# A two-layer pixel-scatter layer on one core: the index stage's lists searched in half rows, its passes fused, some moved to ScalarE

## The chip, the cores and the metric

One Trainium2 chip, one core. The time is the device time of one execution in microseconds, the median of the runs named. Lower is better.

## The reference

Input x is (4, 64, 400, 400), float32. Two layers of the same form follow one another, with their own 1x1 weights. Of one layer:

```python
center = einsum('nchw,oc->nohw', feature, w_center)          # 2 maps
step = relu(einsum('nchw,oc->nohw', feature, w_step))        # 2 maps
prob = sigmoid(einsum('nchw,oc->nohw', feature, w_prob))     # 1 map
offset = transpose(center * step, (0, 2, 3, 1))
th = minimum(round(gh[None] + offset[..., 0]), h - 1)
tw = minimum(round(gw[None] + offset[..., 1]), w - 1)
tgt = mod((th * w + tw).reshape(n, h * w).astype(int32), h * w)
sample = vmap(lambda idx: grid_flat.at[idx].set(grid_flat))(tgt)
sampled = grid_sample_bilinear(feature, scaled(sample))
proped = sampled * prob + feature * (1 - prob)
out = feature * prob + proped * (1 - prob)
```

Each pixel names a target; a target keeps the last pixel that names it, a pixel that nobody names keeps itself. A pixel whose kept source is not itself is called moved. The output is feature + z (sampled - feature) with z = prob (1 - prob).

## The kernel before, in words

The images go in pairs, two images of 64 channels on 128 partitions. A pair of one layer is numbered u = 0 to 3. For each u three things are done. *Tabling* turns the pixels into rows of channels in a table in HBM (TensorE transposes at L1333, ScalarE copies them out at L1397), blends the grid lines that rounding moves (columns on VectorE or GpSimd at L1049 to L1062, rows on VectorE at L1121 to L1139), and computes the five 1x1 maps (L1319). *Indexing*, `indices(u, cuts)`, turns the maps into sources. *Mixing* loads the sampled pixels, transposes them back (L1293), subtracts the feature (L1283) and has VectorE multiply by z and add (L1103, L1105), one image row at a time. Six sweeps run one after another:

| stage | mixes | tables | indexes | from us | to us |
|---|---|---|---|---|---|
| 0 | - | 0 | - | 0 | 545 |
| 1 | - | 1 | 0 | 545 | 1500 |
| 2 | 0 | 2 | 1 | 1500 | 2960 |
| 3 | 1 | 3 | 2 | 2960 | 4640 |
| 4 | 2 | - | 3 | 4640 | 6380 |
| 5 | 3 | - | - | 6380 | 7465 |

A sweep goes over 50 tiles of 8 image rows. The index work of an engine is a Python generator: after each image row of the sweep the engine's program takes `pace` steps of it (0.5, 1, 1.15, 1.15 in stages 1 to 4), so the order on each queue is fixed when the program is built, and work that takes fewer steps ends at an earlier image row. `piece` is one instruction and a step; `pieces(op)` is `cuts` instructions with a step after each (one over 3200 elements in stage 1, two over 1600 in stages 2 to 4); `blanks(n)` is n empty steps; `step` is an instruction without a step of the generator. Every such instruction raises s_v, and the next waits for it.

The index work of one u on VectorE, in order:

- the gate, L483 to L490: z from the last map (Sigmoid and Square on ScalarE, L787 and L790), split into three bfloat16 parts that ScalarE then stores;
- the targets, L493 to L526: maps to target rows and columns, number of the target, distance from the pixel; `code` for targets within R rows and columns (R is 1 in layer 0 and 5 in layer 1), s1m for those further off;
- the near search, L541 and L548, with TensorE, and the far search, a loop on the chip of as many rounds as the fullest partition needs (L578, L579, L622 and others);
- the join, L657 to L676: one source for each pixel. In layer 0 (`sparse`) all moved pixels go to the rounds below;
- in layer 1 the *selection*, L690 to L703: the moved pixels of each image row are picked into 128 slots, eight by eight, the ones that themselves moved away first, by MAX and MATCH_REPLACE. ScalarE and TensorE make row lists and masks of them;
- what is left goes to `keys(1)` and a loop of rounds (L745 on), at the end of which stands the mark "moved"; behind it GpSimd gathers the moved pixels (L916), stores them, and puts them at their places in the table (L940).

If a pixel that itself moved away is left over, a flag makes GpSimd copy the whole table. Behind "moved" VectorE takes over the column blends from GpSimd for a time (`owned`). SyncE issues the first loads of the next stage once `s_path` says that GpSimd is done (L1205 on). In stages 4 and 5 GpSimd also fetches the listed pixels of each image row (L1249), VectorE masks them (L1083), and ScalarE makes one-hot rows (L1431, L1436) beside the gate copy (L1422).

## Time and profile before

| what | value |
|---|---|
| median of 3 runs | 7504.88 us (7486.66 to 7507.91) |
| profiled execution, its own time | 7467.07 us |
| its span | 7465.5 us |
| busy: TensorE, VectorE, ScalarE, GpSimd | 68%, 71%, 41%, 55% |
| TensorE's mean granted clock | 0.834 |

Engines are named PE (TensorE), PEld (its weight loads), DVE (VectorE), ACT (ScalarE), POOL (GpSimd), SP (SyncE). L12 is line 12 of the kernel before. A busy time is the time in which an engine had an instruction running; two that overlap in its pipeline count once there, while the mean duration of a group counts each in full.

### The profile page before, as it was taken

Reading aid. Unit: us, or ns where it says so; the run is one execution under the profiler, and the core shown is the slowest. Engines: PE = TensorE matmul, PEld = TensorE weight load, DVE = VectorE, ACT = ScalarE, POOL = GpSimd, SP = SyncE. Lnnn points to the kernel's source line nnn. Section 1 sums busy time; section 2 is a strip of 40 time slices with the busy share of each in tenths; the row PEclk is TensorE's granted clock in tenths of the full one; section 3 lists DMA queues with packets and bytes.
Section 4 is the critical chain, followed back from the end, with each engine's and each line's share of the span. In section 5 each row is a group of like instructions: output and inputs, shape, how many; then the busy total and the mean of one; then the engine's idle time right before and its main releaser. Section 6 shows DMA issues by size and latency. Waiting matters only on the chain. (4 is left out here: it accounts for less than half of the span.)

```text
span 7465.5 us, 92049 instructions
## 1 busy us (share of the span) xinstructions
PE 5108.6 (68%) x26404; PEld 2886.7 (39%) x26404; DVE 5269.5 (71%) x12387; ACT 3045.9 (41%) x5830; POOL 4128.5 (55%) x8124
## 2 busy tenths in 40 slices
PE   5763554346765677568957666679957646788888
PEld 3442333223443444345634334335533223344444
DVE  7538577267776643777789963778889964687777
ACT  3442222222232333222302323767706647566666
POOL 6657653446363464554506426765516436677776
PEclk8876776677887888789978877889979878899999
DMA  7995666667586888676715778776606566787887
GB/s 279 348 341 181 219 214 217 205 208 248 185 279 204 280 291 288 222 234 220 266 38 205 242 244 272 214 205 196 194 18 186 167 148 209 231 253 256 260 263 233
DMA packets 543222, 1672.98 MB, mean 224 GB/s; under 512 B 125182, under 2 KB 180339, under 8 KB 501012
## 3 DMA queue, kind: packets, MB, share of 16 engines
q1 hardware_dynamic: 223708, 827.34, 35.8%
q10 hardware_dynamic: 254552, 763.42, 27.2%
q0 software_dynamic: 64480, 76.57, 5.5%
q8 instruction: 208, 3.41, 0.2%
q14 instruction: 274, 2.24, 0.1%
HBM read 949.39 MB, written 727.71 MB: 225 GB/s over the span
## 5 line engine op out<-in xcount | busy, mean ns | idle before, releaser
L1103 DVE TENSOR_TENSOR ps<-ps,arena 128x400 f32<-128x400 f32 x1600 | 927.8, 580 | 1409.1 <-PE ps L1293 859.2
L1049 POOL TENSOR_TENSOR arena<-arena 128x32 f32<-128x32 f32 (+8 forms) x3013 | 973.7, 364 | 1537.2 <-PE ps L1319 1528.7
L1283 PE MATMUL ps<-arena,minus 128*128 128x400 f32 x3200 | 1600.1, 585 | 240.1 <-DVE arena L1105 226.6
L1422 ACT ACTIVATE arena<-ps 128x400 f32<-128x400 f32 x1600 | 798.0, 499 | 2185.2 <-PE ps L1269 1037.0
L1333 PE MATMUL ps<-ident,arena 128*128 128x128 f32 x5000 | 906.5, 328 | 840.9 <-ACT arena L1397 529.4
L1249 POOL DMA_INDIRECT arena<-table,gidx x800 | 887.3, 1109 | 697.3 <-PE ps L1302 457.5
L1397 ACT ACTIVATE arena<-ps 128x512 f32<-128x512 f32 (+1 forms) x1400 | 734.6, 552 | 1231.6 <-PE ps L1333 608.5
L1333 PEld LDWEIGHTS ps<-ident,arena 128*128 128x128 f32 x5000 | 737.2, 203 | 1026.3 <-ACT arena L1397 618.7
L1302 PE MATMUL ps<-arena 128*64 128x400 f32 x3200 | 767.6, 559 | 468.6 <-ACT arena L1436 197.9
L1293 PEld LDWEIGHTS ps<-ident,arena 100*128 100x128 f32 x6400 | 768.4, 150 | 640.6 <-issue 474.6
L1249 POOL DMA_INDIRECT arena<-table,arena x800 | 820.6, 1026 | 268.4 <-issue 239.4
L1105 DVE TENSOR_TENSOR arena<-arena,ps 128x400 f32<-128x400 f32 x1600 | 913.5, 571 | 55.2
L1293 PE MATMUL ps<-ident,arena 100*128 100x100 f32 x6400 | 890.6, 265 | 76.7 <-DMA arena<-table 72.9
L1062 POOL TENSOR_TENSOR arena<-arena 128x32 f32<-128x32 f32 (+8 forms) x3013 | 867.6, 333 | 121.2 <-DMA y<-arena 114.8
L1283 PEld LDWEIGHTS ps<-arena,minus 128*128 128x128 f32 x3200 | 548.0, 209 | 760.9 <-issue 422.7
L1269 PE MATMUL ps<-arena,halves 128*128 128x400 bf16 x1600 | 578.7, 362 | 292.8 <-ACT arena L1422 188.5
L1436 ACT ACTIVATE arena<-arena,one 128x400 f32<-128x400 f32 x1200 | 706.5, 622 | 13.1
L1431 ACT ACTIVATE arena<-grid,gcol 128x400 f32<-128x400 f32 x800 | 457.7, 622 | 283.0 <-PE ps L1302 193.3
L1049 DVE TENSOR_TENSOR arena<-arena 128x32 f32<-128x32 f32 (+8 forms) x1587 | 248.1, 233 | 373.2 <-PE ps L1319 362.9
L1319 PE MATMUL ps<-arena,w_conv 128*32 128x400 f32 x3200 | 421.9, 631 | 95.1 <-DMA arena<-x 70.7
L847 PE MATMUL ps<-arena,ident 100*100 100x400 bf16 x2080 | 411.8, 341 | 30.4 <-DVE arena L541 30.4
L1269 PEld LDWEIGHTS ps<-arena,halves 128*128 128x128 bf16 x1600 | 167.4, 105 | 631.4 <-issue 216.3
(214 smaller groups left out, 5859.5 us busy)
## 6 DMA issues: line engine op xcount, KB each, us to landing
arena<-x SPq DMA_DIRECT2D x200, 1600.0 KB, 10.8
arena<-table SPq DMA_DIRECT2D x400, 800.0 KB
table<-arena ACTq DMA_DIRECT2D x400, 512.0 KB, 5.1
y<-arena ACTq DMA_DIRECT2D x200, 800.0 KB, 9.1
arena<-y SPq DMA_DIRECT2D x100, 1600.0 KB, 14.2
out<-arena ACTq DMA_DIRECT2D x200, 800.0 KB
table<-arena ACTq DMA_DIRECT2D x200, 576.0 KB, 10.5
conv<-arena ACTq DMA_DIRECT2D x800, 31.2 KB
```

The costliest lines, as they stand in the source:

```text
L1049: last = E.tensor_tensor(tmp[:, :, at:at + size], cols[:, :, y + to:end + to:step], cols[:, :, y:end:step], ALU.subtract)
L1062: last = E.tensor_tensor(cols[:, :, y:end:step], cols[:, :, y:end:step], tmp[:, :, at:at + size], ALU.add)
L1103: V.tensor_tensor(d, d, g, ALU.mult).then_inc(s_mix, 1)
L1105: V.tensor_tensor(y, y, d, ALU.add).then_inc(s_y, 1)
L1249: pool.indirect_dma_start(got[:, m % DEPTH, e * C:(e + 1) * C], None, rows, bass.IndirectOffsetOnAxis(ap=gidx[:, 2 * m + e:2 * m + e + 1], ...
L1269: nc.tensor.matmul(ps[:, 6 + m % GB, 0:W], halves[:, m % HALF * 128:(m % HALF + 1) * 128], gates_all[j % RR], start=True, stop=True).then_ ...
L1283: nc.tensor.matmul(ps[:, sums(r), 0:W], minus[:, :], tile(t)[:, r * W:(r + 1) * W], start=True, stop=False)
L1293: last = nc.tensor.matmul(ps[:, sums(r), q * STRIP:(q + 1) * STRIP], s_rows[j % RR][:, q, m % HALF, :], ident[0:STRIP, 0:STRIP], is_transp ...
L1302: last = nc.tensor.matmul(ps[e * C:(e + 1) * C, sums(r), 0:W], got[:, m % DEPTH, e * C:(e + 1) * C], oneh[m % 2][:, e, :], start=False, st ...
L1333: last = nc.tensor.transpose(ps[:, 2 + count % 2, j * PX:(j + 1) * PX], pixels[:, j0 + j, :], ident[:, :])
L1397: nc.scalar.activation(t_out[nth % TR][:, (j0 - at) * CH2:(j0 - at + size) * CH2], ps[:, 2 + count % 2, 0:size * PX], ACT.Copy).then_inc(s ...
L1422: nc.scalar.activation(gate[m % 2], ps[:, 6 + m % GB, 0:W], ACT.Copy).then_inc(s_gcopy, 1)
```

## The change

Four things are done. In the selection, seven of nine turns search the two halves of an image row apart, each for its own eight largest, and two turns search the whole row; before, 16 turns searched the whole row. The slots are the same 128. A step now comes after 1600 elements of MAX or MATCH_REPLACE, as before. The gate's first pass and its three roundings to bfloat16 go to ScalarE, with empty steps on VectorE while it works. The squares of the two distances go to ScalarE; VectorE takes their maximum and compares it where it forms `code` and s1m. Other passes are fused in pairs; the numbers kept in s0m and c1m are larger by one for a part of the way.

```diff
-TURNS = SLOTS // 8
+HALVED = 7
+TURNS = [(16 * t, W // 2) for t in range(HALVED)] + [(8 * t, W) for t in range(2 * HALVED, SLOTS // 8)]
...
-                dve.wait_ge(s_zact, 2 * u + 2)
-                yield from pieces(lambda c, r: V.tensor_scalar(z[:, c], z[:, c], 0.25, -1.0, ALU.subtract, ALU.mult))
                 parts = [t.bitcast(BF16) for t in (near, *hit)]
-                yield from pieces(lambda c, r: V.tensor_copy(parts[0][:, c], z[:, c]))
-                yield from pieces(lambda c, r: V.tensor_tensor(z[:, c], z[:, c], parts[0][:, c], ALU.subtract))
-                yield from pieces(lambda c, r: V.tensor_copy(parts[1][:, c], z[:, c]))
-                yield from pieces(lambda c, r: V.tensor_tensor(z[:, c], z[:, c], parts[1][:, c], ALU.subtract))
-                yield from pieces(lambda c, r: V.tensor_copy(parts[2][:, c], z[:, c]), "gate")
+                for a in range(2):
+                    dve.wait_ge(s_zact, 6 * u + 4 + a)
+                    yield from pieces(lambda c, r: V.tensor_tensor(z[:, c], z[:, c], parts[a][:, c], ALU.subtract), f"rest{a}")
+                    yield from blanks(3 * cuts)
...
-                yield from pieces(lambda c, r: V.tensor_scalar(c1m[:, c], c1m[:, c], MAGIC, None, ALU.add))
                 yield from pieces(lambda c, r: V.tensor_scalar(c0m[:, c], c0m[:, c], MAGIC, float(W), ALU.add, ALU.mult))
-                yield from pieces(lambda c, r: V.tensor_tensor(s0m[:, c], c0m[:, c], c1m[:, c], ALU.add))
+                yield from pieces(lambda c, r: V.scalar_tensor_tensor(s0m[:, c], c1m[:, c], MAGIC, c0m[:, c], ALU.add, ALU.add))
...
-                yield from pieces(lambda c, r: V.tensor_tensor(m3(c1m)[:, r], m3(c1m)[:, r], gcols[:, r], ALU.subtract))
-                yield from pieces(lambda c, r: V.tensor_tensor(s1m[:, c], c0m[:, c], c0m[:, c], ALU.mult))
-                yield from pieces(lambda c, r: V.tensor_scalar(s1m[:, c], s1m[:, c], float(R * R), None, ALU.is_le))
-                yield from pieces(lambda c, r: V.tensor_tensor(z[:, c], c1m[:, c], c1m[:, c], ALU.mult))
-                yield from pieces(lambda c, r: V.scalar_tensor_tensor(z[:, c], z[:, c], float(R * R), s1m[:, c], ALU.is_le, ALU.mult))
+                yield from pieces(lambda c, r: V.scalar_tensor_tensor(m3(c1m)[:, r], m3(c1m)[:, r], 1.0, gcols[:, r], ALU.subtract, ALU.subtract), "moves")
+                yield from blanks(3 * cuts)
+                dve.wait_ge(s_square, 2 * u + 2)
+                yield from pieces(lambda c, r: V.tensor_tensor(z[:, c], z[:, c], s1m[:, c], ALU.max))
...
+                yield from pieces(lambda c, r: V.scalar_tensor_tensor(s1m[:, c], z[:, c], float(R * R), s0m[:, c], ALU.is_gt, ALU.mult), "far")
                 dve.wait_ge(s_gatest, (u + 1) * 16 * 6)
-                yield from pieces(lambda c, r: V.tensor_tensor(code[:, c], c0m[:, c], z[:, c], ALU.mult), "code")
-                yield from pieces(lambda c, r: V.tensor_scalar(z[:, c], z[:, c], -1.0, 1.0, ALU.mult, ALU.add))
-                step(V.scalar_tensor_tensor(s1m, s0m, 1.0, z, ALU.add, ALU.mult), "far")
+                yield from pieces(lambda c, r: V.scalar_tensor_tensor(code[:, c], z[:, c], float(R * R), c0m[:, c], ALU.is_le, ALU.mult), "code")
...
-                yield from pieces(lambda c, r: V.scalar_tensor_tensor(c1m[:, c], c0m[:, c], -float(SIDE), near[:, c], ALU.mult, ALU.add))
-                yield from pieces(lambda c, r: V.scalar_tensor_tensor(c1m[:, c], c0m[:, c], float(W), c1m[:, c], ALU.mult, ALU.add))
+                yield from pieces(lambda c, r: V.scalar_tensor_tensor(c1m[:, c], c0m[:, c], float(W - SIDE), near[:, c], ALU.mult, ALU.add))
...
-                yield from pieces(lambda c, r: V.tensor_scalar(c0m[:, c], c1m[:, c], 0.0, None, ALU.is_equal))
-                yield from pieces(lambda c, r: V.scalar_tensor_tensor(c0m[:, c], s0m[:, c], 1.0, c0m[:, c], ALU.add, ALU.mult))
-                yield from pieces(lambda c, r: V.scalar_tensor_tensor(c1m[:, c], c1m[:, c], -1.0, c0m[:, c], ALU.add, ALU.add))
+                yield from pieces(lambda c, r: V.scalar_tensor_tensor(c0m[:, c], c1m[:, c], 0.0, s0m[:, c], ALU.is_equal, ALU.mult))
+                yield from pieces(lambda c, r: V.scalar_tensor_tensor(c1m[:, c], c1m[:, c], 1.0, c0m[:, c], ALU.subtract, ALU.max))
                 if sparse:
-                    yield from pieces(lambda c, r: V.tensor_tensor(c0m[:, c], c1m[:, c], s0m[:, c], ALU.subtract))
-                    yield from pieces(lambda c, r: V.tensor_scalar(c0m[:, c], c0m[:, c], 0.0, None, ALU.is_equal))
-                    yield from pieces(lambda c, r: V.tensor_scalar(c0m[:, c], c0m[:, c], -1.0, 1.0, ALU.mult, ALU.add))
+                    yield from pieces(lambda c, r: V.tensor_tensor(c0m[:, c], c1m[:, c], s0m[:, c], ALU.not_equal))
...
+                    taken = {}
+                    for at, width in TURNS:
+                        for kind in range(2):
+                            done = 0
+                            for j in range(BROWS):
+                                for a in range(W // width):
+                                    top8 = tops[:, j * SLOTS + at + 8 * a:j * SLOTS + at + 8 * a + 8]
+                                    among = s1m[:, j * W + a * width:j * W + (a + 1) * width]
...
+                                        note(V.max(top8, among))
...
+                                        note(V.match_replace(among, top8, among, 0.0))
...
+                                if done >= 4 * W or j == BROWS - 1:
+                                    done = 0
+                                    yield
...
+                act.wait_ge(s_zact, 6 * u + 2)
+                nc.scalar.activation(z, z, ACT.Relu, bias=quarter[0:NB, 0:1], scale=-1.0).then_inc(s_zact, 1)
+                yield
+                act.wait_ge(s_zact, 6 * u + 3)
+                for a, t in enumerate((near, *hit)):
+                    if a:
+                        yield from after(act, clock, f"rest{a - 1}")
+                    nc.scalar.activation(t.bitcast(BF16), z, ACT.Copy).then_inc(s_zact, 1)
...
+                yield from after(act, clock, "moves")
+                nc.scalar.activation(s1m, c0m, ACT.Square).then_inc(s_square, 1)
+                nc.scalar.activation(z, c1m, ACT.Square).then_inc(s_square, 1)
```

In the program that this makes, an image row of stage 3 on VectorE is L1103 and L1105 (L1116 and L1118 after). Before, the selection began in image row 244:

```order
L695 MAX arena<-arena 100x8 x4
L1103 TENSOR_TENSOR ps<-ps,arena 128x400
L1105 TENSOR_TENSOR arena<-arena,ps 128x400
L695 MAX arena<-arena 100x8 x4
L1103 TENSOR_TENSOR ps<-ps,arena 128x400
L1105 TENSOR_TENSOR arena<-arena,ps 128x400
L700 MATCH_REPLACE arena<-arena 100x400 x4
L1103 TENSOR_TENSOR ps<-ps,arena 128x400
L1105 TENSOR_TENSOR arena<-arena,ps 128x400
L700 MATCH_REPLACE arena<-arena 100x400 x4
L695 MAX arena<-arena 100x8 x4
```

Now it begins in image row 242, with eight MAX or MATCH_REPLACE over half rows (`x8`) where four over whole rows stood:

```order
L695 MAX arena<-arena 100x8 x8
L1116 TENSOR_TENSOR ps<-ps,arena 128x400
L1118 TENSOR_TENSOR arena<-arena,ps 128x400
L1140 TENSOR_SCALAR arena<-arena 128x400 x2
L1152 SCALAR_TENSOR_TENSOR arena<-arena 128x400 x2
L695 MAX arena<-arena 100x8 x8
L1116 TENSOR_TENSOR ps<-ps,arena 128x400
L1118 TENSOR_TENSOR arena<-arena,ps 128x400
L699 MATCH_REPLACE arena<-arena 100x200 x8
L1116 TENSOR_TENSOR ps<-ps,arena 128x400
L1118 TENSOR_TENSOR arena<-arena,ps 128x400
```

The last MATCH_REPLACE stood in image row 299 and stands in 273; "moved" stood in 330 and stands in 304. In stage 4 it is the same, in stage 2 "moved" goes from image row 185 to 179.

The squares in stage 4, VectorE before (L516 to L518 are the squares and a comparison, L1083 masks an image row's pixels):

```order
L516 TENSOR_TENSOR arena<-arena 100x1600
L1083 TENSOR_TENSOR arena<-arena,keep 100x4x128
L1103 TENSOR_TENSOR ps<-ps,arena 128x400
L1105 TENSOR_TENSOR arena<-arena,ps 128x400
L517 TENSOR_SCALAR arena<-arena 100x1600 x2
L1083 TENSOR_TENSOR arena<-arena,keep 100x4x128
L1103 TENSOR_TENSOR ps<-ps,arena 128x400
L1105 TENSOR_TENSOR arena<-arena,ps 128x400
L518 TENSOR_TENSOR arena<-arena 100x1600
L1083 TENSOR_TENSOR arena<-arena,keep 100x4x128
L1103 TENSOR_TENSOR ps<-ps,arena 128x400
```

and now, where seven image rows with nothing of the index work in them stand between L515 and L518:

```order
L515 SCALAR_TENSOR_TENSOR arena<-arena,grid 100x1600
L1096 TENSOR_TENSOR arena<-arena,keep 100x4x128
L1116 TENSOR_TENSOR ps<-ps,arena 128x400
L1118 TENSOR_TENSOR arena<-arena,ps 128x400
L1096 TENSOR_TENSOR arena<-arena,keep 100x4x128
L1116 TENSOR_TENSOR ps<-ps,arena 128x400
L1118 TENSOR_TENSOR arena<-arena,ps 128x400
L1096 TENSOR_TENSOR arena<-arena,keep 100x4x128
...
L1116 TENSOR_TENSOR ps<-ps,arena 128x400
L1118 TENSOR_TENSOR arena<-arena,ps 128x400
L518 TENSOR_TENSOR arena<-arena 100x1600
```

On ScalarE the two squares (L807, L808) stand together between the gate copy of one image row (L1435) and the one-hot rows of the next (L1444, L1449):

```order
L1444 ACTIVATE arena<-grid,gcol 128x400 x2
L1449 ACTIVATE arena<-arena,one 128x400 x2
L1435 ACTIVATE arena<-ps 128x400
L807 ACTIVATE arena<-arena 100x3200
L808 ACTIVATE arena<-arena 100x3200
L1444 ACTIVATE arena<-grid,gcol 128x400 x2
L1449 ACTIVATE arena<-arena,one 128x400 x2
L1435 ACTIVATE arena<-ps 128x400
```

Before, ScalarE had none but its own work of the image rows there.

## Rows read from the trace of the kernel before

**Rows 1.** Busy us (and instructions) by stage: PE, PEld, DVE, ACT, POOL; clock, DMA

```profile
0.00:545.00 545.00, 348.67 (x2102) 221.95 (x2102) 289.70 (x1401) 234.56 (x458) 344.58 (x1179) 0.81 0.87 325
545.00:1500.00 955.00, 412.03 (x2308) 263.49 (x2304) 596.66 (x1994) 239.20 (x456) 535.67 (x1084) 0.68 0.63 206
```

**Rows 2.** The same for stretches inside stages 3 and 4

```profile
4068.00:4273.00 205.00, 139.18 (x686) 79.04 (x686) 202.91 (x519) 60.31 (x122) 91.91 (x340) 0.82 0.69 236
4504.00:4554.00 50.00, 41.33 (x232) 23.40 (x231) 22.84 (x40) 19.18 (x39) 36.60 (x147) 0.89 0.91 312
4756.00:4885.00 129.00, 96.93 (x450) 44.99 (x449) 127.42 (x168) 103.18 (x200) 106.23 (x75) 0.96 0.73 223
5735.00:5975.00 240.00, 159.99 (x660) 70.39 (x660) 237.90 (x570) 156.17 (x300) 129.47 (x131) 0.89 0.59 173
6271.00:6325.00 54.00, 48.57 (x231) 22.84 (x229) 34.78 (x60) 49.67 (x101) 41.20 (x43) 0.95 0.75 229
```

**Rows 3.** Line 1103 alone, one instruction for each image row: busy (count)

```profile
4068.00:4273.00 205.00, 31.95 (x57) 0.82 0.69 236
4504.00:4554.00 50.00, 11.46 (x20) 0.89 0.91 312
5735.00:5975.00 240.00, 34.80 (x61) 0.89 0.59 173
6271.00:6325.00 54.00, 11.31 (x20) 0.95 0.75 229
```

**Rows 4.** Timeline, stage 1's end: start us, us, engine, line, operation

```profile
1184.04 0.06 DVE L773 MEMSET arena<- 128x2 f32 x1 [0.24 <-DVE arena L771]
...
1421.08 4.21 PE L1333 MATMUL ps<-ident,arena 128*128 128x128 f32 x17 [4.78 <-ACT arena L1397]
...
1503.83 0.32 SPq L1178 DMA_DIRECT2D arena<-gate  x1
```

**Rows 5.** Timeline, VectorE, selection of stage 4

```profile
5830.87 2.00 DVE L695 MAX8 arena<-arena 100x8 f32<-100x400 f32 x4
5832.79 0.68 DVE L1083 TENSOR_TENSOR arena<-arena,keep 100x512 f32<-100x512 f32 x1
...
5838.15 0.56 DVE L700 MATCH_REPLACE8 arena<-arena 100x400 f32<-100x400 f32 x1
...
5838.70 0.56 DVE L700 MATCH_REPLACE8 arena<-arena 100x400 f32<-100x400 f32 x1
```

**Rows 6.** Groups by line and shape, VectorE: busy us, mean ns, idle before

```profile
L695 DVE MAX8 arena<-arena 100x8 f32<-100x400 f32 x256 | 127.9, 562 | 0.0
...
L578 DVE MAX8 arena<-arena 128x8 f32<-128x1250 f32 x36 | 52.7, 1465 | 14.6 <-DVE arena L572 5.8 <-DVE arena L771 3.0 <-DVE arena L650 2.1
...
L516 DVE TENSOR_TENSOR arena<-arena 100x1600 f32<-100x1600 f32 x6 | 11.3, 1880 | 0.0
...
L504 DVE TENSOR_SCALAR arena<-arena 100x1600 f32<-100x1600 f32 x6 | 6.1, 1016 | 0.0
```

**Rows 7.** Groups by line and shape, ScalarE

```profile
L790 ACT ACTIVATE arena<-arena,half 100x3200 f32<-100x3200 f32 x4 | 11.8, 2955 | 0.0
```

**Rows 8.** Timeline, VectorE, the wait for the maps in stage 1

```profile
584.00 1.83 DVE L490 CAST arena<-arena 100x3200 bf16<-100x3200 f32 x1
598.00 3.49 DVE L493 SCALAR_TENSOR_TENSOR arena<-arena 100x3200 f32<-100x3200 f32 x1 [12.17 <-DMA arena<-conv]
```

**Rows 9.** Timeline, GpSimd, first blend of stage 0 and of stage 1

```profile
32.94 5.13 POOL L1049 TENSOR_TENSOR arena<-arena 128x80 f32<-128x80 f32 x23 [32.24 <-PE ps L1319]
...
568.36 19.59 POOL L1049 TENSOR_TENSOR arena<-arena 128x80 f32<-128x80 f32 x23 [7.04 <-PE ps L1319]
```

**Rows 10.** Line 916 alone, gathers of moved pixels by stage: busy (count)

```profile
545.00:1500.00 955.00, 72.31 (x64) 0.68 0.63 206
...
2960.00:4640.00 1680.00, 16.36 (x16) 0.84 0.65 216
4640.00:6380.00 1740.00, 16.01 (x16) 0.88 0.58 170
```

34 lines of the change are left out of this document (16 added, 18 removed).

## The prediction

> **What bounds the kernel now.** I read the busy table by stage first, then stretches inside the stages, then the timeline where a stage begins or ends. Stage 0 needs 545 us for its 50 tiles, 10.9 us a tile; stage 1 does the same to the second table and needs 955 us, because the index work of pair 0 lies on the same queues [rows 1]. So index work costs time even where an engine's average is low: VectorE is busy for 597 of stage 1's 955 us [rows 1].
>
> The stretches say when. In the selection of stage 3 VectorE is busy for 202.9 of 205 us, in that of stage 4 for 237.9 of 240, in the first passes of stage 4 for 127.4 of 129 [rows 2]: VectorE alone is the bound there. Where no index work is left, 50 us hold 20 image rows in stage 3 (2.5 us each) and 54 us hold 20 in stage 4 (2.7 us), with VectorE at 46% and 64% [rows 2, 3]. An image row has two prices then: VectorE's work in it, or a floor set by others (transfers at 0.91 in stage 3, ScalarE at 49.7 of 54 us in stage 4 [rows 2]). I take floors of 2.65 and 2.7 us, since stage 3's first free image rows, with the scatter still running, are dearer.
>
> Stage 1 ends otherwise. VectorE's last index instruction is at 1184.0; GpSimd then gathers and scatters the moved pixels in rounds; TensorE's last transposes begin at 1421.1; SyncE may issue stage 2's first loads only at 1503.8 [rows 4]. For the last 78 us nothing but that scatter runs. Whatever brings the index work's end forward brings stage 2 forward, up to those 78 us.
>
> **The selection (stages 3 and 4).** Before, 16 turns of 8 MAX and 8 MATCH_REPLACE over 400 elements, 128 of each a stage. Four MAX start within 5830.87 to 5832.79, 0.48 us apart though each lasts 0.56; two replacements start 0.55 apart, the value load included [rows 5]. That makes 128 x 0.476 + 128 x 0.544 = 131 us a stage. MAX lasts 562 ns for 400 elements and 1465 for 1250 [rows 6]: 1.06 ns an element, so 200 elements save 0.21 us each, whatever the constant part. After, 112 of each are over halves and 16 over whole image rows: 2 x 112 x 0.21 = **47 us less a stage**, 84 left.
>
> That is not all gain. The steps fall from 64 to 36; at 1.15 steps an image row this empties 24.3 image rows. Stage 3 before: 57 image rows in 205 us [rows 2, 3], 3.6 each, so 201 us for the selection's 56; less its own 131 us, VectorE's other work is 1.26 us an image row. After: 31.5 x 1.26 + 84 = 124 us; 77 less, but the 24.3 image rows now cost their floor, 64 us: **13 us gained**. Stage 4: 61 in 240 us, 3.93 each, 220 for the 56, other work 1.6: 31.5 x 1.6 + 84 = 134; 86 less, minus 24.3 x 2.7 = 66: **20 us gained**. The two halves of the change partly undo each other: the work shrinks by 47 us, but it leaves sooner the image rows in whose slack it could lie.
>
> **Passes fused or moved.** A pass over the 3200 elements of a partition, in two pieces, costs 2 x 1.02 us with one operand and 2 x 1.88 with two [rows 6]. Gone behind the gate: the separate adding of MAGIC (2.0), two squares and a comparison (9.6), 1-z (2.0): 13.7 us a stage. Gone after the far list: one two-operand pass and one of one operand, about 6 us; in the sparse stages 1 and 2 two more of one operand, 10. The gate loses four one-operand passes, 8.8 us.
> - Stage 3, front: 13.7 us less, but six empty steps (5.2 image rows) stand where the squares were, where VectorE's 1.26 falls under the floor: 6 to 7 us lost. I take 7. After the far list: 6 us less, 3.5 image rows emptied at 1.4 us: 1 to 2, I take 2. The gate lies where loads bound the stage's first image rows: 0. Sum 9.
> - Stage 2: the same front, 6; after the far list 2. Sum 8.
> - Stage 4: ScalarE is busy for 103.2 of 129 us in the front [rows 2] and gets two squares, back to back, of 2.96 us each [rows 7]. Over the 5.2 image rows of the six steps it has 5.2 x 2.5 + 5.9 = 18.9 us, where VectorE had 5.2 x 1.6 + 9.6 = 17.9. So the squares are worth nothing there, the gate's copies nothing or 2 us the wrong way, the rest 3. Sum 2.
> - Stage 1: a pass is one instruction of both pieces. The gate's own passes were hidden: VectorE waits 12.2 us for the convolution maps until 598.0 [rows 8]; the longer chain on ScalarE (two more activations, 6 us, before the first subtraction) fits in that. A pass costs 1.83 us with one operand, 3.49 with two [rows 8]: from the map wait on three of the first kind and two of the second go in the front, 12.5 us; three and one behind the far list, 9.0. VectorE is busy for 0.62 of the stage, for more where passes follow one another; I count four fifths, 17 us. The order shows the last index step 3 steps earlier, and 2 of them were added ahead of the map wait, in idle time: 5 steps, 10 image rows, 1.25 tiles at 10.9, 14 us. **31 us**, all on the path through GpSimd's rounds.
>
> GpSimd's tile blend is the other engine's half of the front: 23 subtractions took 5.1 us beside VectorE's short blend operations, 19.6 us beside its passes [rows 9]. I book nothing for it. The Trainium skill, page SBUF — State Buffer, section SBUF: two separate sides, says why: a VectorE operation with two SBUF inputs, or in a two-port mode, holds a port pair that GpSimd needs, for the whole instruction. Rows 9 agree in size, though they cannot show a lock. By that rule each pass taken off VectorE also frees GpSimd; this is the second rival.
>
> **Sum**: 31 + 8 + (13 + 9) + (20 + 2) = **83 us**. Against the profiled execution's own 7467 us that is 7384; the median of the runs shown, 7504.88, lies 38 us above it, and I predict against the median: **7420** (7505 - 83, rounded). A measurement here tells 0.3%, 22 us, from no change.
>
> **Rivals.**
> 1. *The squeeze costs more.* The emptied image rows cost 3.0 rather than 2.65, and ScalarE holds up stage 4 for each of its six added passes (6 x 2.96 = 18 us). For it: ScalarE at 0.8 there. Against: two of the six fall in image rows that wait for loads. Minus 17 (48.6 x 0.35) and 18: gain 48, 7457. Chance 0.2.
> 2. *GpSimd is freed too.* By rows 9 a blend's subtractions beside passes are 14 us slower. Some 30 blends of GpSimd's lie in the fronts of stages 1 to 3, and there 35 passes become 26, a quarter fewer: 30 x 14 x 0.25 = 105 us of GpSimd's, of which I put under half on the path, 45 us: 7375. Chance 0.2.
> 3. *Halves cost as much as wholes.* Then the 2 x 47 us are not there and the squeeze is: 83 - 94 = -11, 7516. The Trainium skill, VectorE: DVE Perf Modes, section on the TRN2 errata, warns that small tiles pay a fixed cost for each instruction and advises 512 elements or more. Rows 6 hold the fixed part of a MAX of 400 to 137 of 562 ns, so this stays at 0.03.
> 4. *Slower: the lists overflow.* A half that has over 56 moved pixels must share the last 16 slots; what is left goes to the rounds of gather and scatter, where a round has 16 gathers: stages 3 and 4 have one each, stage 1 has four [rows 10]. In stage 1 the four take from 1184.0 to 1503.8 [rows 4], 80 us a round. In stage 4 GpSimd also fetches each image row, so a second round adds those 80 there, in stage 3 perhaps half: 7420 + 120 = 7540. It decides as soon as one partition has more than 8 pixels left. Worked out from the reference on its inputs: 54 moved pixels in a half on average, 77 at most, and at most 6 left in a partition under either scheme; no pixel is left that sets the flag for copying a whole table. Chance 0.03.
>
> **How the numbers follow.** Forecast 0.54, rivals as given. The predicted time is the forecast's. The range takes in rivals 1 and 2 with the noise of the runs (21 us between the three shown): 7360 to 7470, leaving out 3, 4 and the outer ends. Faster by over 0.3% holds for the forecast and both first rivals less their weak ends: 0.91; within 0.3% 0.05; slower 0.04.
>
> **What would show it.** MAX and MATCH_REPLACE over 200 elements at 0.35 us; the last MATCH_REPLACE of stage 3 in image row 273 instead of 299; the selection's 130 us denser, at 4 us an image row; stage 1's last index instruction near 1152 and stage 2's first load 32 us sooner; four rounds in stages 1 and 2, one in 3 and 4. If stages 3 and 4 gain over 40 us each, the floor in the emptied image rows was too high; if stage 1 gains nothing, its end hangs on something else. Wrong altogether if stage 4 grows.

## The result and the profile after

The changed kernel takes **7434.5 us** (median of five runs, 7427.2 to 7441.1); the kernel before, run beside it, 7488.4 (five runs, 7477.3 to 7507.9, the three known before among them). The ratio is **0.9923, with an interval of 0.9908 to 0.9939**: 46 to 69 us faster. The prediction was 7420 against a median of 7505, that is 83 us of gain; by the ratio 58 came, seven tenths of them. The time lies in the range, 14 us above the forecast. Part of that nearness is luck: against the 7488 of the five runs the same 83 us would have given 7405.

The profiled execution of after has a span of 7432.7 us, 33 less than before's. Before's two profiled executions on this chip (7467 and 7473 us) both lie under all its other runs there, after's (7434 and 7431) lie among its own. So the stages below add up to some 20 us less gain than the medians show; which stage holds those 20 us no profile tells.

The busy table by stage (mixing starts at the window borders; columns as in [rows 1]), first the kernel before, one line for each of the five stages:

```profile
0.00:1512.00 1512.00, 763.26 (x4412) 486.58 (x4413) 886.36 (x3393) 474.77 (x916) 880.25 (x2263) 0.72 0.72 248
1512.00:2965.00 1453.00, 950.92 (x5140) 569.67 (x5139) 903.40 (x1970) 432.22 (x857) 746.48 (x1977) 0.82 0.75 251
2965.00:4659.00 1694.00, 1195.11 (x6473) 743.90 (x6472) 1268.74 (x2685) 440.06 (x867) 774.76 (x2262) 0.84 0.65 216
4659.00:6399.00 1740.00, 1261.07 (x5996) 649.66 (x5995) 1368.29 (x2747) 1036.20 (x1998) 919.41 (x836) 0.88 0.59 171
6399.00:7466.00 1067.00, 938.25 (x4390) 436.94 (x4388) 842.70 (x1593) 662.62 (x1194) 807.57 (x788) 0.94 0.79 252
```

and the changed kernel:

```profile
0.00:1475.00 1475.00, 766.79 (x4413) 491.64 (x4414) 858.61 (x3381) 491.60 (x922) 862.78 (x2263) 0.73 0.73 254
1475.00:2942.00 1467.00, 952.37 (x5139) 568.16 (x5138) 873.72 (x1945) 448.45 (x863) 704.57 (x1977) 0.83 0.75 249
2942.00:4638.00 1696.00, 1199.19 (x6472) 747.17 (x6470) 1204.07 (x2663) 457.01 (x872) 778.25 (x2262) 0.83 0.64 216
4638.00:6369.00 1731.00, 1262.78 (x5999) 650.49 (x5998) 1299.37 (x2727) 1049.68 (x2005) 903.27 (x836) 0.87 0.58 172
6369.00:7433.00 1064.00, 938.59 (x4388) 436.37 (x4386) 842.70 (x1593) 663.85 (x1194) 808.21 (x787) 0.94 0.80 253
```

The first line of each holds stages 0 and 1. VectorE's busy time falls by 28, 30, 65 and 69 us in stages 1 to 4, 191 us in all, and the stages change by **-37, +14, +2 and -9**. Almost all of the gain is in the stage where VectorE's saving was smallest. That is the thing to explain. (These are one profile of each kernel; the +14 does not come again below.)

Stage 1's end, in the timeline; it answers to [rows 4]:

```profile
1144.30 0.06 DVE L774 MEMSET arena<- 128x2 f32 x1 [0.24 <-DVE arena L772]
...
1466.91 0.32 SPq L1191 DMA_DIRECT2D arena<-gate  x1
```

VectorE's last index instruction is 40 us earlier, stage 2's first load 37 us. The selection's instructions, by line and shape, answer to the first of [rows 6]; the last row is the replacements of before, the others are after's:

```profile
L699 DVE MATCH_REPLACE8 arena<-arena 100x200 f32<-100x200 f32 x224 | 75.5, 349 | 0.0
L695 DVE MAX8 arena<-arena 100x8 f32<-100x200 f32 x224 | 62.4, 351 | 0.0
L699 DVE MATCH_REPLACE8 arena<-arena 100x400 f32<-100x400 f32 x32 | 17.5, 558 | 0.0
L695 DVE MAX8 arena<-arena 100x8 f32<-100x400 f32 x32 | 15.8, 558 | 0.0
```
```profile
L700 DVE MATCH_REPLACE8 arena<-arena 100x400 f32<-100x400 f32 x256 | 140.1, 559 | 0.0
```

0.35 us for half the elements where the whole takes 0.56: the 0.21 us that the prediction used. And the stretches of 35 image rows from image row 240 on, in stage 3 and in stage 4, which answer to the selection's in [rows 2], with two more lines for later: image rows 40 to 80 of stage 3, and 210 to 220 of stage 4.

```profile
4050.00:4190.00 140.00, 93.10 (x412) 52.29 (x413) 138.62 (x482) 36.13 (x73) 61.22 (x212) 0.75 0.62 217
5726.00:5874.00 148.00, 97.42 (x380) 41.29 (x379) 146.76 (x493) 90.84 (x175) 70.95 (x71) 0.85 0.54 156
3115.00:3278.00 163.00, 99.19 (x487) 58.30 (x480) 110.45 (x164) 48.33 (x88) 96.99 (x235) 0.72 0.69 235
5616.00:5659.00 43.00, 30.84 (x136) 14.12 (x134) 30.73 (x41) 27.50 (x54) 30.91 (x24) 0.88 0.87 245
```

The first two: VectorE at 99%, 4.0 and 4.2 us an image row, as the prediction had it ("denser, at 4 us an image row"). The same two places of the kernel before, image rows 40 to 80 of stage 3 and 210 to 220 of stage 4:

```profile
3138.00:3291.00 153.00, 92.94 (x478) 55.01 (x476) 115.06 (x167) 42.68 (x86) 98.35 (x235) 0.77 0.71 248
5638.00:5671.00 33.00, 26.09 (x128) 12.41 (x126) 32.62 (x42) 28.99 (x58) 25.07 (x17) 1.00 0.81 244
```

With less of VectorE's work in both, they take 10 us more each. In the first VectorE was at 0.75, so it was no bound there; in the second it was at 0.99 and is at 0.71 now: something else stops it.

### The profile page after: what moved, and what is told of

It is laid out like the page before. It is cut to its first block and busy times, and to the rows that moved or that the text cites. A ratio compares the mean times of both kernels' runs of the same rounds, so it can differ in the third digit from the quotient of the medians.

```text
span 7432.7 us, 91994 instructions
## 1 busy us (share of the span) xinstructions
PE 5119.7 (69%) x26404; PEld 2893.8 (39%) x26404; DVE 5078.5 (68%) x12308; ACT 3110.6 (42%) x5854; POOL 4057.1 (55%) x8124
## 3 DMA queue, kind: packets, MB, share of 16 engines
q8 instruction: 208, 3.41, 0.2%
## 5 line engine op out<-in xcount | busy, mean ns | idle before, releaser
L1116 DVE TENSOR_TENSOR ps<-ps,arena 128x400 f32<-128x400 f32 x1600 | 927.5, 580 | 1536.1 <-PE ps L1306 967.0
L1062 POOL TENSOR_TENSOR arena<-arena 128x32 f32<-128x32 f32 (+8 forms) x3013 | 926.6, 347 | 1603.6 <-PE ps L1332 1593.3
L1435 ACT ACTIVATE arena<-ps 128x400 f32<-128x400 f32 x1600 | 797.9, 499 | 2116.8 <-PE ps L1282 1068.8
L1262 POOL DMA_INDIRECT arena<-table,gidx x800 | 870.3, 1088 | 698.9 <-PE ps L1315 459.4
L1118 DVE TENSOR_TENSOR arena<-arena,ps 128x400 f32<-128x400 f32 x1600 | 913.2, 571 | 55.3
L1075 POOL TENSOR_TENSOR arena<-arena 128x32 f32<-128x32 f32 (+8 forms) x3013 | 856.4, 329 | 119.3 <-DMA y<-arena 113.0
L1449 ACT ACTIVATE arena<-arena,one 128x400 f32<-128x400 f32 x1200 | 706.7, 622 | 13.1
L1444 ACT ACTIVATE arena<-grid,gcol 128x400 f32<-128x400 f32 x800 | 458.0, 623 | 282.0 <-PE ps L1315 200.3
```

The costliest lines, as they stand in the source:

```text
L1062: last = E.tensor_tensor(tmp[:, :, at:at + size], cols[:, :, y + to:end + to:step], cols[:, :, y:end:step], ALU.subtract)
L1075: last = E.tensor_tensor(cols[:, :, y:end:step], cols[:, :, y:end:step], tmp[:, :, at:at + size], ALU.add)
L1116: V.tensor_tensor(d, d, g, ALU.mult).then_inc(s_mix, 1)
L1118: V.tensor_tensor(y, y, d, ALU.add).then_inc(s_y, 1)
L1262: pool.indirect_dma_start(got[:, m % DEPTH, e * C:(e + 1) * C], None, rows, bass.IndirectOffsetOnAxis(ap=gidx[:, 2 * m + e:2 * m + e + 1], ...
L1435: nc.scalar.activation(gate[m % 2], ps[:, 6 + m % GB, 0:W], ACT.Copy).then_inc(s_gcopy, 1)
```

## The experiments

Where experiments are compared by image row, the figure is the time from one image row's mixing to another's in the trace, divided by their number. In stages 3 and 4 it repeats well: image rows 200 to 240 of stage 4 took 8.39 and 8.42 us in two executions of before, 8.68 and 8.68 in two of after. The kernels ran on three chips, called A (the result's own), B and C here; absolute times are compared on one chip alone.

### Both kernels once more (chip A)

No edit.

> The kernel before, unchanged, once more. Purpose: how far a stage's length moves from one execution to the next, since the differences to be explained are 2 to 37 us a stage. Both theories: stage lengths (start of one stage's first tile to the next's) within 5 us of the first profile, the whole within 25 us. If a stage moves by over 10 us, differences of that size in stages 2 to 4 say nothing by themselves.

> The changed kernel, unchanged, once more, for the same purpose: stage lengths within 5 us of its first profile. The growth of stage 2 by 14 us against the kernel before must come again if it belongs to the change; if it is within 5 us of before this time it was chance.

Measured, length of stages 0 and 1 together, then of stages 2 to 5:

```
before        1512.6  1452.7  1693.4  1740.5  1061.2
before_again  1509.1  1464.1  1700.4  1735.6  1057.2
after         1475.5  1466.9  1695.9  1730.4  1059.1
after_again   1479.0  1454.4  1700.8  1728.7  1061.0
```

Stage 2 moves by 11 to 13 us from one execution to the next in both kernels, so its growth by 14 us is not shown to belong to the change: the means are 1458.4 and 1460.7. The others, by means: stage 1 shorter by 33.6, stage 3 longer by 1.4, stage 4 shorter by 8.5. The expectation of 5 us of spread was too tight for stages 2 and 3.

### Only the selection in half rows (chip A)

```
+HALVED = 7
-TURNS = SLOTS // 8
+TURNS = [(16 * t, W // 2) for t in range(HALVED)] + [(8 * t, W) for t in range(2 * HALVED, SLOTS // 8)]
...
(the loop over TURNS as in the change; nothing else of it)
```

> The kernel before with only the selection in half rows. Theory A (the prediction's terms for the selection are right, those for the fronts of stages 2 to 4 are not): stages 1 and 2 unchanged, stage 3 shorter by 13 us, stage 4 by 20 us, the whole by about 33 us (ratio 0.9956). Rival B (the 33 us are the profile's chance, halves cost as much as wholes): no gain, or slower by 10 us. Rival C (the emptied image rows cost nothing extra, VectorE's 47 us a stage all count): 94 us less, ratio 0.987.

Measured: 7456.4 us beside 7491.4, ratio 0.995 (0.9934 to 0.9966), 25 to 49 us less. In the whole theory A holds; B (no gain) and C (94 us) are out. By stage it holds in stage 4 alone: the stages are 1514.0, 1465.4, 1693.1 and 1720.4 us, against before's means stage 4 is shorter by 18 (20 expected) and stage 3 by 4 (13 expected). Image rows 240 to 400 of stage 3 take 10 us less, and its first 240, whose code is that of before, 2 and 10 us more than in before's two executions. By image row, before against this kernel: stage 3, rows 240 to 280 3.73 and 3.94; 280 to 320 3.57 and 4.03; **320 to 360 3.86 and 2.88**. Stage 4: 4.02 and 4.23, 3.84 and 4.74, **5.53 and 3.87**. The selection's image rows are dearer with half the work in each instruction, and the ones behind it cheap: the work shrinks, and the image rows that it leaves are paid at their own price.

```profile
4082.00:4221.00 139.00, 91.64 (x407) 51.64 (x408) 137.66 (x481) 36.07 (x73) 63.75 (x212) 0.76 0.64 220
5751.00:5901.00 150.00, 96.38 (x385) 41.22 (x385) 148.80 (x495) 90.49 (x175) 78.39 (x79) 0.86 0.56 162
```

The same 35 image rows as in after's table, within 2 us of them, so this part acts alone as it does in the whole.

### Everything but the half rows (chip A)

```
-HALVED = 7
+HALVED = 0
```

> The changed kernel with every selection turn over whole image rows again: fused passes, the gate's roundings and the squares stay as changed. Theory A (only stage 1's passes lie on a path; in the fronts of stages 2 to 4 an image row has a floor of 3 us or more, set by others than VectorE): stage 1 shorter by 31 to 37 us, stage 2 to 4 between 0 and 14 us longer each, the whole shorter by 15 to 30 us. Rival (the prediction's terms for the fronts hold, and the first profile hid them): stage 1 shorter by 31, stage 2 by 8, 3 by 9, 4 by 2, the whole by 50 us, ratio 0.9933.

Measured: 7464.4 us, ratio 0.9955 (0.9939 to 0.9971), 22 to 46 us less. Its stages in its one profile are 1478.5, 1456.2, 1709.9, 1754.3, 1060.4: against before's means stage 1 is shorter by 32, stage 2 by 2, **stage 3 is longer by 13 and stage 4 by 16**. So the passes fused and moved pay in stage 1 and cost in the others; the rival's 19 us in stages 2 to 4 are not there. By image row the largest losses are where the table above found them: rows 40 to 80 of stage 3 (4.03 for 3.84, 8 us) and rows 200 to 240 of stage 4 (8.70 for 8.4, 12 us); in stage 3 another 5 us lie in rows 80 to 120. The first 200 rows of stage 4 take 4 to 7 us more.

Both parts together, 37 and 34 us by their ratios, are 71; the change has 58 (46 to 69), which agrees within the intervals.

### Two empty steps less (chip B)

What VectorE waited for in image rows 210 to 220 of stage 4, after (engine, line, what it waited for: us in total, times, longest); before has no such wait there:

```profile
DVE arena L1096 <- DMA arena<-table: 11.6, 2, 8.6
```

The timeline of the place, after, VectorE and then SyncE's queue. L658 and L659 are passes behind the far list, L842 (below) is the read-back of the far lists, L1192 a load of four image rows' pixels, L1212 the load of a new tile:

```profile
5648.31 1.82 DVE L659 SCALAR_TENSOR_TENSOR arena<-arena 100x1600 f32<-100x1600 f32 x1
5658.71 0.69 DVE L1096 TENSOR_TENSOR arena<-arena,keep 100x512 f32<-100x512 f32 x1 [8.58 <-DMA arena<-table]
```
```profile
5642.80 0.31 SPq L1192 DMA_DIRECT2D arena<-table  x1
5643.60 4.30 SPq L1212 DMA_DIRECT2D arena<-y  x1
```
```profile
5637.52 0.73 ACTq L842 DMA_DIRECT2D arena<-farsrc  x2
```

The tile load takes SyncE 4.3 us to issue and lands 27.9 us later; the pixels' load issued 0.8 us ahead of it is waited for until 5658.7, 16 us, and VectorE stands for 8.6 us, and with it ScalarE (8.9) and TensorE (7.6). In the kernel before the far table is written in image row 208 of the stage and read back in 214; the changed front has two steps more, and it is 210 and 216, where a tile ends and the next is loaded. The experiment takes the two steps out again, elsewhere:

```
                 for a in range(2):
                     ...
-                    yield from blanks(3 * cuts)
+                    yield from blanks(3 * cuts - (cuts == 2))
```

> The changed kernel with two of its empty steps before the convolution maps taken out in stages 2 to 4, so that the far table's write falls in image row 208 of the stage again, as before, not 210. In stage 4 the kernels with the changed front stand still for about 10 us near image row 216, where the read-back of the far lists, the load of a new tile and the image row's own load are issued together. Theory A (the phase of that read-back against the tile loads costs it): image rows 200 to 240 of stage 4 take 8.4 us each again, not 8.7, so stage 4 is 10 us shorter than in the changed kernel. Rival (a pass less between the write and the read-back costs it, whatever the image row): no difference in those image rows.

Measured: image rows 200 to 240 of stage 4 take **8.45 us**, in the other kernels of the same series 8.68 and 8.73. That is 8 to 11 us, nearly the whole loss, and the pass that is missing between write and read-back is missing here too: theory A, the rival is out. (Which of the transfers holds up which is read from the times of issue; no run separates them.) The wait is gone from the table of waits (0.3 us in place of 11.6):

```profile
DVE arena L1096 <- DMA arena<-table: 0.3, 1, 0.3
```

and the transfers stand apart, ScalarE's read-back 9.5 us behind the tile load instead of 6 ahead of it (in the kernel before it was 9.5 behind, too):

```profile
5698.65 0.40 SPq L1212 DMA_DIRECT2D arena<-y  x1
```
```profile
5708.11 0.31 ACTq L842 DMA_DIRECT2D arena<-farsrc  x1
```

In stage 3 rows 40 to 80 went back to 3.85 us as well, with rows 0 to 40 at 4.42 in place of 4.3: 1 to 4 us to the good over the 80 rows.

### The squares on VectorE again (chip B)

```
-                yield from blanks(3 * cuts)
-                dve.wait_ge(s_square, 2 * u + 2)
+                yield from pieces(lambda c, r: V.tensor_tensor(s1m[:, c], c0m[:, c], c0m[:, c], ALU.mult))
+                yield from pieces(lambda c, r: V.tensor_tensor(z[:, c], c1m[:, c], c1m[:, c], ALU.mult))
+                yield from blanks(cuts)
...
(ScalarE: the wait for "moves" and the two Square activations are taken out)
```

> The changed kernel with the two squares on VectorE again, four instructions of 1.9 us in the place of the six empty steps and the wait for ScalarE; the number of steps is the same. The prediction's term: the squares off VectorE gain 3 to 4 us in stages 2 and 3 (9.6 us of work less the six steps' 6), so this kernel is 3 us a stage slower there. Theory A, from the rows of the first profiles (image rows 40 to 80 of stage 3 take 4.0 us each with the empty steps, 3.84 before): the empty steps hide nothing and this kernel is 0 to 3 us a stage quicker in image rows 40 to 80. Stage 4: no difference within 3 us. The 10 us stall near image row 216 of stage 4 stays, since no step is moved.

Measured: image rows 40 to 80 of stage 3 take 3.93 us. The changed kernel had 4.06, 4.01 and 3.97 in three executions, on chips A and C, and three other kernels whose code is the same there had 3.99, 4.02 (chip B) and 3.94 (chip C). With 6.5 us *more* of work these image rows take 0 to 5 us less: the prediction's 3 us do not show, and the sign is theory A's, though the lowest of the six is only 0.01 us above. In stage 2 rows 40 to 80 show 3.40 for 3.41, and the first 200 rows of stage 4 are within 2 us of the kernels beside it that have the same steps. The stall near image row 216 stayed (8.73), as expected. **Stage 1 is another matter**, and nothing was expected of it: its last index instruction comes at 1154.2, where the three kernels beside this one, with the same code in stages 0 and 1 as the changed kernel, have 1150.0, 1150.0 and 1145.4. There the squares off VectorE seem to be worth 4 to 9 us.

```profile
3168.00:3326.00 158.00, 91.47 (x489) 54.31 (x489) 117.00 (x168) 42.78 (x86) 99.55 (x235) 0.78 0.72 244
```

This is the same 40 image rows as in after's third line above: 117.0 us of VectorE's in 158, where after has 110.5 in 163.

### No slots left over (chip B)

```
-HALVED = 7
+HALVED = 8
```

> The changed kernel with all eight turns over half rows, so that no slots are left for a half with more than 64 moved pixels: it puts a price on the prediction's fourth rival. By the reference some 105 to 120 pixels of an image are then left to the rounds of gather and scatter, at most 17 in a partition for the first pair of the second layer and 13 for the second pair: three rounds there and two, where one is needed now. The prediction's price is 80 us a round where GpSimd also fetches the image rows and half of that in stage 3: stage 3 longer by 80 (two rounds at 40), stage 4 by 80. Rival (a round costs the 200 us by which GpSimd's row fetches stand still in one round now): stage 3 about 100 to 200 longer, stage 4 200 longer. The selection itself: 16 MAX and 16 replacements of 400 become 32 and 32 of 200 in time 0.35 each, 5 us more a stage.

Measured: 7965.9 us. Stage 3 takes 1839 us, where its neighbours in the series have 1681 to 1702, stage 4 1891 where the two with the dense selection have 1819 and 1825. GpSimd's gathers of moved pixels, by stage (busy, count), in groups of 16:

```profile
2975.00:4816.00 1841.00, 46.63 (x48) 0.80 0.61 200
4816.00:6707.00 1891.00, 32.04 (x32) 0.84 0.55 158
```

Three rounds and two, as counted from the inputs. Two more rounds cost stage 3 some 140 us, one more costs stage 4 some 70, 5 of it the selection's own: **65 to 70 us a round in either stage**. The prediction's 80 was near for stage 4; its half price for stage 3 was wrong. The rival's 200 was wrong for stage 4; its 100 to 200 for stage 3 held the 140, but not for its reason, since a round costs the same in both stages. Each is one execution. So the seven half turns and two whole ones are a choice with a cliff next to it.

### Five more empty steps in stage 1 (chip C)

```
-                    yield from blanks(2 * BLANKS + 4)
+                    yield from blanks(2 * BLANKS + 4 + (5 if u == 0 else 0))
```

> The changed kernel with five more empty steps at the end of stage 1's index work, before the rounds: it prices a step of stage 1 by itself. The prediction: a step is two image rows, eight make a tile of 10.9 us... five steps are 10 image rows, 1.25 tiles, 14 us later for the last index instruction and for stage 2's first tile, since GpSimd's rounds lie between. Rival (a step costs only what VectorE does in it, or GpSimd's rounds have slack): under 4 us. Stages 2 to 5 as in the changed kernel.

Measured beside the changed kernel on the same chip. The changed kernel:

```profile
1143.69 0.06 DVE L774 MEMSET arena<- 128x2 f32 x1 [0.24 <-DVE arena L772]
...
1302.35 0.95 POOL L929 DMA_INDIRECT arena<-table,arena  x1 [0.30 <-issue]
...
1464.38 0.32 SPq L1191 DMA_DIRECT2D arena<-gate  x1
```

and with the five steps:

```profile
1167.27 0.06 DVE L774 MEMSET arena<- 128x2 f32 x1 [0.24 <-DVE arena L772]
...
1317.54 0.95 POOL L929 DMA_INDIRECT arena<-table,arena  x1 [0.30 <-issue]
...
1472.94 0.32 SPq L1191 DMA_DIRECT2D arena<-gate  x1
```

The last index instruction is 23.6 us later, the last gather 15.2, stage 2's first load 8.6. The first is well beyond chance: with the changed kernel's code it came between 1143 and 1150 us in all seven other executions. So five steps delay VectorE by more than 14 us. The prediction priced a tile of stage 1 at stage 0's 10.9 us; at stage 1's own mean, 955 us for 50 tiles, 10 image rows are 24 us. The 8.6 us at the end are not shown to be an effect: three kernels with identical code in stages 0 and 1 had stage 2's first load at 1447.8, 1457.6 and 1466.9 us on chip B. In the change 40 us on VectorE arrived as 37 in one pair of profiles and 30 in the other. How much of a delay arrives is open.

### The half rows in 64 steps (chip B)

```
-                                if done >= 4 * W or j == BROWS - 1:
+                                if done >= (4 * W if width == W else 2 * W) or j == BROWS - 1:
```

> The changed kernel, with the selection in half rows cut into 64 steps again, as before, instead of 36: the same instructions, spread over as many image rows as before. Theory A (the halves give 47 us of VectorE's work a stage, and 33 of the 94 arrive only because the steps are dense): the work leaves evenly, an image row of the selection takes (201-47)/56 = 2.75 us in stage 3 and (220-47)/56 = 3.1 in stage 4, so 47 us a stage less than before, where the changed kernel had 13 and 20: another 61 us, the whole near 7375. Rival (image rows that are not full of index work have a floor of about 3.5 us in these stretches, set by others): 0 to 15 us less than the changed kernel. Rival 2 (the index chain's end lies before the stage's end by too little when it comes 24 image rows later): slower than the changed kernel.

Measured: 7732.6 us beside 7794.1 of before, ratio 0.9913 (0.9894 to 0.9932). The changed kernel itself wasn't in this series; its two neighbours with the dense selection had 7788.6 and 7782.0, one run each. The 59 image rows from 240 on, stage 3 and stage 4, in this kernel, in 64 steps:

```profile
4090.00:4267.00 177.00, 132.75 (x699) 77.65 (x700) 165.97 (x529) 61.72 (x124) 92.39 (x350) 0.87 0.81 286
5791.00:5990.00 199.00, 153.45 (x644) 68.80 (x643) 186.41 (x565) 150.31 (x295) 124.44 (x121) 0.88 0.67 199
```

and in the changed kernel on chip C, in 36:

```profile
4090.00:4311.00 221.00, 152.88 (x747) 89.15 (x747) 206.63 (x561) 61.30 (x124) 105.67 (x349) 0.78 0.70 238
5805.00:6044.00 239.00, 160.49 (x681) 72.49 (x681) 225.86 (x598) 151.17 (x292) 116.46 (x110) 0.86 0.59 175
```

3.0 us an image row instead of 3.75, 3.4 instead of 4.05: 44 and 40 us. Against before on chip C, which takes 213 and 238 us for these 59 rows, it is 36 and 39 us less, where theory A has 47. It isn't kept whole. The round of gather and scatter now falls into image rows 320 to 360, which take 4.16 and 6.22 us, where the dense selection's have 2.9 and 3.7 to 4.3. From image row 240 to the stage's end 20 and 24 us are left in stage 3 and 34 and 20 in stage 4 (chip B, against the two neighbours): 54 and 45 us, most of theory A's 61 and far more than the first rival's 15. The ratio to before is another matter: theory A's 7375 is 0.985, and 0.9913 is no better than the changed kernel's own on chip A. The next series says why.

### Three choices altered together (chip C)

The two-step edit, the squares on VectorE and the 64 steps, as in the three diffs above, beside both kernels once more.

> The kernel before once more, as the reference of this series by stage and image row, since the series with the 64 steps ran on a chip where every kernel takes 4% longer (before 7794 us there). Both theories: image rows 200 to 240 of stage 4 at 8.4 us each, rows 240 to 320 of stages 3 and 4 at 3.65 and 3.9.

> The changed kernel once more, timed in one series with the version below. Ratio to before 0.992 again (0.9908 to 0.9939 the first time), and stage 4's image rows 200 to 240 at 8.7 us each.

> The changed kernel with three of its choices altered: the selection in half rows in 64 steps, two empty steps less before the maps in stages 2 to 4, and the squares on VectorE. From the runs so far, image rows 240 to 400 against the changed kernel: stage 3 about 21 to 27 us less, stage 4 20 to 34 less, rows 200 to 240 of stage 4 10 less, the squares 3 us less in stage 3. Theory A: 55 to 75 us less than the changed kernel, ratio to before 0.983 to 0.985. Rival (what the dense selection loses is given back by the round of gather and scatter, which now ends 24 image rows later, in the last fifth of the stage): under 30 us less than the changed kernel, ratio over 0.988.

Measured on this chip: before 7753.6 us (17 runs); the changed kernel **7737.2**, ratio **0.9974** (0.9957 to 0.9991); the three together **7656.0**, ratio **0.988** (0.9855 to 0.9905), its six runs (7633 to 7701) all below the changed kernel's twelve (7712 to 7755). Two things follow.

The version beats both kernels: 81 us less than the changed kernel by the medians, more than theory A's 55 to 75, and 37 by the profiled executions, of which this kernel's was its slowest. Its ratio to before is not the expected 0.984, because the changed kernel fell short of its own. Image rows 200 to 240 of stage 4 are at 8.42 again (8.69 in the changed kernel beside it). Its stages 3 and 4, and then the changed kernel's, on chip C:

```profile
2985.00:4664.00 1679.00, 1191.96 (x6472) 747.02 (x6471) 1213.71 (x2667) 450.37 (x870) 778.08 (x2261) 0.84 0.65 218
4664.00:6447.00 1783.00, 1269.59 (x5998) 652.92 (x5996) 1301.86 (x2730) 1040.66 (x2002) 919.19 (x837) 0.86 0.57 167
```
```profile
2985.00:4684.00 1699.00, 1198.63 (x6471) 747.01 (x6471) 1203.33 (x2664) 456.75 (x872) 782.04 (x2262) 0.84 0.64 215
4684.00:6506.00 1822.00, 1290.54 (x5997) 660.55 (x5997) 1297.61 (x2727) 1046.33 (x2005) 910.88 (x837) 0.86 0.56 164
```

With 10 and 4 us more of VectorE's work the stages are 20 and 39 us shorter. What counts there is where the work stands, not how much of it there is. By image row, behind row 240 stage 3 is 22 us shorter and stage 4 27, which is the 64 steps; in front of it stage 4 is 12 us shorter, which is the stall; the first 240 rows of stage 3 are not shorter (1107 us for 1105). The squares back on VectorE are not seen to bring anything, and in stage 1 they cost: its last index instruction is 11 us later (1154.5 for 1143.7) and stage 2's first load 14 us later (1478.0 for 1464.4).

And the change is worth 0.8% on chip A but 0.3% on chip C, from the same code. On C stage 1 is 49 us shorter, stage 2 12 longer, stage 3 1 shorter, and stage 4, which had gained 9 on A, is 21 us *longer*: 18 us in its first 200 image rows, 11 in the stall, and only 8 gained behind image row 240, where A has 22. These are single executions: another kernel on C whose code is the same in stage 4 had 1811 us, 10 longer than before and not 21. Why these image rows are dearer on C is open.

## Why the prediction was right, and where not

**The selection: right.** Its step was 47 us less work a stage, 24.3 image rows emptied at a floor of 2.65 or 2.7, 13 and 20 us gained. Image rows 240 to 400 of stage 4 gained 22 and 21 us in the two pairs of profiles; those of stage 3 gained 13 and 4, and 10 with the selection alone, so the 13 are confirmed in sign and rough size only. By itself the selection brings 25 to 49 us where 33 were forecast. The 64 steps confirm the form of the sum too: with the image rows not emptied most of the rest of the 47 us is there, and a good part of it arrives.

**Stage 1: right in size, not in its parts.** 31 forecast, 34 measured (means of two profiles each, 37 and 30). The working split it into 17 us of passes and 14 of steps; five steps alone moved the last index instruction by 23.6 us. It also let every microsecond arrive: the last index instruction was to come 32 us sooner and came 39 to 40 sooner, of which 30 to 37 arrived. So the sum was near while a step's price was not; two errors of opposite sign lie in it, and that it came out within 3 us is in part luck.

**The fronts and the far lists of stages 2 to 4: wrong.** The failed step is "*6 to 7 us lost. I take 7. After the far list ... I take 2 ... Sum 9*" with its likes in stages 2 (8) and 4 (2), 19 us in all (13.7 us less 6 to 7 lost to the emptied image rows leaves the 7 counted as gain). It costed VectorE's work as if VectorE bound each of these image rows, down to the floor read in stretches free of index work. The only front shown in the rows of before was stage 4's, with VectorE at 127.4 of 129 us [rows 2]; in image rows 40 to 80 of stage 3 it is at 0.75 (115 of 153 us), and they take 3.8 us, far over the floor of 2.65. Work taken out of image rows that VectorE doesn't bound brought nothing here. That the six empty steps with a wait on ScalarE made them dearer is likely (0 to 5 us less without them) and not shown. The passes cost stages 3 and 4 13 and 16 us instead of bringing 9 and 2; in the changed kernel itself, whose first 240 image rows hold no selection, these rows take 10 and 13 us more than before's, by means of two profiles each.

**A wait of which the prediction had none.** Some ten of stage 4's lost 16 us are the stall at image row 216. The prediction counted what the added steps do to VectorE's image rows, and had costed the edit for the gate as hidden; it did not ask at which image row the transfers behind them are now issued. Of a shift by two image rows the price was not in VectorE's work but in the transfers that then met.

**The rivals.** The first had two halves. Emptied image rows at 3.0 us isn't what stage 3 shows, where rows 320 to 360, behind the selection, cost 2.76 us; in stage 4 the same rows cost 3.95, well over the 2.7 of the floor, though before's cost 5.53 there, so that the stage gains all the same. ScalarE's 18 us in stage 4 are not there: without the selection's change its first 200 image rows take 4 to 7 us more. The second: GpSimd is indeed quicker (the first blend of stage 1 takes 11.7 us for 19.6 in [rows 9]; its busy time falls by 42 us in stage 2 in the first pair of profiles and 31 in the second), and stage 2 is not a microsecond shorter by the means, so that side of the sharing had slack. Its rule, in the Trainium skill, page SBUF — State Buffer, section SBUF: two separate sides, agrees with those rows. It agrees instruction by instruction too, which the merged [rows 9] could not show: a subtraction of GpSimd's that starts with a VectorE pass of 3.49 us in the kernel before lasts 3.57 and ends 0.1 us behind it, and one of the same shape behind the passes lasts 0.24 (below, under the first blend of after). The third (halves as dear as wholes) is out, 0.35 against 0.56 us. The fourth did not occur: one round each in stages 3 and 4, and its price is 65 to 70 us a round, not 80 and 40.

```profile
575.08 11.70 POOL L1062 TENSOR_TENSOR arena<-arena 128x80 f32<-128x80 f32 x23 [14.19 <-PE ps L1332]
```
```profile
580.47 3.49 DVE L489 TENSOR_TENSOR arena<-arena 100x3200 f32<-100x3200 f32 x1
580.49 3.57 POOL L1049 TENSOR_TENSOR arena<-arena 128x32 f32<-128x32 f32 x1
...
585.88 0.24 POOL L1049 TENSOR_TENSOR arena<-arena 128x32 f32<-128x32 f32 x1
```

**The sum.** 83 forecast, 58 measured. By the stages of two profiles each it is 38: stage 1 has 3 more than forecast, stage 2 lacks 10, stage 3 23, stage 4 14. The 19 of the failed step, what the fronts lost on top of it and the stall's 10 more than cover the missing 25; which stage gives back the 20 us between profiles and medians is not known, so no closer account can be had. That the median of before fell from 7504.9 to 7488.4 with two more runs shows how wide three runs are.

**Open**: why image rows 40 to 80 of stage 3 become dearer by 0.2 us with less work in them (the two steps more are part of it: without them 3.85); why the kernels take 4% longer on chips B and C, and why the change is worth less there; how a delay of stage 1's last index instruction passes through the rounds; and which of the transfers around image row 216 holds up the others.

## What to carry to other kernels

Before costing work taken off an engine, read that engine's busy share in the very stretch where the work stands, not in the stretch next to it: 191 us came off VectorE here, and the gain came where it was the bound or where the chain behind it set a stage's end; 65 and 69 us less work in stages 3 and 4 made them 1 us longer and 9 shorter. When a schedule counts in steps, an edit has three prices: the work, the steps that it empties, and the transfers that it shifts against others. Three small edits of where work stands brought 81 us by the medians on a chip where the change itself had brought some 20; by the image rows it was the same instructions over more steps and one read-back moved by two image rows, while the two squares given back to VectorE cost stage 1 something and gained nothing visible.

## What the runs showed of the hardware

- The same program with the same inputs takes 4% longer on two of three chips: 7754 and 7794 us for 7490. Before's stage 3 is as long on chips A and C (1693 to 1700 us), stages 2 and 4 are 35 to 66 us longer on C, and stage 5, where no index work runs, is 15% longer. Chip A's stage 5 stands in the tables above (1067 us, granted clock 0.94, transfers 0.79); the same on chip C:

```profile
6524.00:7750.00 1226.00, 984.88 (x4386) 450.66 (x4386) 833.33 (x1590) 662.47 (x1193) 820.74 (x787) 0.89 0.70 219
```

  The granted clock is 0.89 for 0.94, and TensorE is busy for 985 us for 938. Those 47 us explain less than a third of the 159; nothing in the profile names the rest.
- A tile load of 1.6 MB, issued while GpSimd's fetches and the read-back of the lists were under way, took SyncE 4.3 us to issue and landed after 27.9 us, where before's at the like place took 0.35 and landed after 13.6. The issue repeats: 4.3 to 4.6 us in the six executions looked at with the changed front, on all three chips, and 0.35 to 0.42 in before's two, in the kernel with two steps less and in the one with three choices altered.
- MAX and MATCH_REPLACE of 200 elements cost 0.35 us each, of 400 0.56: a fixed part of about 0.14 us, as worked out for MAX from 400 and 1250 and again from 200 and 400.
- A GpSimd subtraction of 128x32, 0.24 us by itself, lasted 3.57 us beside the VectorE pass of 3.49 us that it started with (lines above). With one such pass beside them the 23 subtractions of stage 1's first blend took 11.7 us, with four passes 19.6.
